# Part one of a fused attention and FFN kernel: one staggered sequence of steps over eight rows in place of two groups of four

## The chip, the cores and the metric

The kernel runs on one core of one Trainium2 chip. A core has five engines with queues of their own: TensorE (matmul, called PE in the profile), VectorE (DVE), ScalarE (ACT), GpSimd (POOL) and SyncE (SP), which here only issues DMAs. The metric is the device time of one execution in microseconds. The kernel before takes 1943.8 us, the median of 3 runs (1938.8 to 1947.53).

## What is computed

The input x has 8 batch rows of 2048 tokens with 256 features. A layer of Nystrom attention (16 heads of 16, 64 landmarks) is followed by a token-shift FFN, each on the layer-normed input and each layer-normed and added back.

```python
q_l = q.reshape(B, H, M, denom, HS).sum(axis=-2) / denom      # landmarks, M = 64
k_l = k.reshape(B, H, M, denom, HS).sum(axis=-2) / denom
s1 = softmax(einsum('bhld,bhmd->bhlm', q, k_l))
s2 = softmax(einsum('bhmd,bhnd->bhmn', q_l, k_l))
s3 = softmax(einsum('bhmd,bhld->bhml', q_l, k))
z = swapaxes(s2) / (max_row_sum * max_col_sum)                # pinv(s2), 6 iterations
for _ in range(6):
    xz = s2 @ z
    z = 0.25 * z @ (13 * I - xz @ (15 * I - xz @ (7 * I - xz)))
out = (s1 @ (z @ (s3 @ v))) @ Wo + bo
```

## The kernel before

The program has two parts. **Part one** makes, for each of the 8 batch rows, the statistics of the layer norm of x, the landmarks of q and k, and the pseudo-inverse of s2. The landmarks and the inverse go to DRAM (`landmarks`, `inverse`). **Part two** goes over the rows again, 4 chunks of 512 tokens each, and computes everything else; its order is written out in the lists `PRO`, `BODY` and `LAST` (line 353 on). The change leaves part two as it is, but for its first steps.

"Row" below means a batch row. Part one takes the rows in two groups of GR = 4 (0 to 3, then 4 to 7). Row n uses set n % 4 of all buffers, with two of the eight PSUM banks, `pb[s][0]` and `pb[s][1]`, and one of three x1in buffers of 2 MB (NX1 = 3), so that a load of x waits for the pooling of the row three before. Within a group every stage is done for all four rows before the next stage begins:

- statistics of x (`st`, 4 quarters of 4 bn_stats each, then `mv` with 16 bn_aggr) on VectorE, the root on ScalarE (`ln`, `rstd`), pooling weights `pw` on VectorE, pooling by 16 matmuls on TensorE;
- the front: norm of the landmarks (`stl`, `mvl`, `xl`), transposes (`lT`, `xlT`), projections (`qk`, `ql`, `kl`, `lm`, `lmlo`), the block-diagonal q (`qbd`, two VectorE multiplies by head_mask, line 939), logits, softmax (`max`, `shift`, `exp`, `sum`, `rcp`, `X`), its transpose (`XT`), row and column sums (`cs` and the reduce at line 961), their maxima over a head (`cm`, `cg`, `cr`, `gb`, `gcol`), and X and XT multiplied by the factor (lines 999 and 1000, `gX`, `gXT`);
- 6 iterations of four phases, S, T2, T3 and Z with ZT. Each product is done in fp16 with high and low parts. ScalarE takes the high part of a PSUM bank (`high`, line 697), VectorE the low part (`low`, line 966), and copies then build the block-diagonal left operand of the next product: `Sbd` and `T3bd` (line 975, two copies of 64 partitions each) on VectorE, `ZTbd` (line 711, two as well) on ScalarE. TensorE multiplies in `product` (line 1243): 24, 48, 32, 24 and 24 matmuls for S, T2, T3, Z and ZT of one row. The last iteration has no Z and no ZTbd.

The statistics of rows 4 to 6 are spread over the iterations of rows 0 to 3 (`AHEAD`). Every engine has a list of steps (`pe_steps`, `act_steps`, `dve_steps`), and each step counts one semaphore of its engine up by one; `of(...)` gives the place in a list, on which the others wait. An engine executes its list strictly in order.

The inverses are written to DRAM from ScalarE's queue at the end of each group (line 728). At the end of part one ScalarE, VectorE and GpSimd wait for all lists that matter to them and for all landmarks and inverses to land in DRAM; SyncE too. TensorE waits only for ScalarE's and VectorE's lists. Then SyncE loads the first x chunks of part two (`stage_X`, line 488), VectorE normalises them (`stage_XA`, line 1046), TensorE transposes (`stage_R`, line 1336), and GpSimd clears buffers and sets the ones row of k_stack in four memsets on one partition (line 616).

Of the kernel before, what the change touches and what calls it, by code (L numbers as in the profile page):

```python
# [6 lines left out]
F16 = mybir.dt.float16  # L7
# [8 lines left out]
def sandwich(nc, x, Wk, Wq, Wv, Wo, bo, W_r, W_k, W_v, mu_r, mu_k, out):  # L16
# [23 lines left out]
    with ctx:  # L40
# [3 lines left out]
        def sem(name):  # L44
# [19 lines left out]
        ident16 = sb("ident16", [P, P], F16)  # L64
        eye7 = sb("eye7", [P, M], F16)
# [74 lines left out]
        p_pooled = sem("p_pooled")  # L140
        p_zero = sem("p_zero")
        p_pe = sem("p_pe")
        p_act = sem("p_act")
        p_dve = sem("p_dve")
        lm_out = sem("lm_out")
        zt_out = sem("zt_out")


        pe_steps = ([(n, s) for n in ("lT", "qk", "logits", "XT", "sums", "g") for s in ROWS]
                    + [(n, i, s) for i in range(ITERS) for names in (["S"], ["T2"], ["T3"], ["Z", "ZT"])  # L150
                       for s in ROWS for n in names if not (n == "Z" and i == ITERS - 1)])
        act_steps = ([(n, s) for names in (["ln", "rstd"], ["xlT"], ["ql", "kl", "lm"], ["exp"], ["XT", "XThi"],
                                           ["Zhi", "ZThi"])
                      for s in ROWS for n in names]
                     + [(n, i, s) for i in range(ITERS) for names in (["S"], ["ZTbd"], ["T2"], ["T3"], ["Z", "ZT"])
                        for s in ROWS for n in names
                        if not (n in ("Z", "ZT", "ZTbd") and i == ITERS - 1)])

        STATS = ([("st", 0), ("st", 1)] + [k for s in range(2, GR) for k in (("pw", s - 2), ("st", s))]
                 + [("pw", GR - 2), ("pw", GR - 1)])  # L160
        FRONT = [(n, s) for names in (["stl", "mvl", "xl"], ["lmlo", "qbd"], ["max", "shift"], ["sum", "rcp", "X", "rs"],
                                      ["cs", "XTlo", "XTbd"], ["cm", "cg", "cr", "gb"], ["gcol", "gX", "gXT"],
                                      ["Zlo", "ZTlo"])
                 for s in ROWS for n in names]
        PHASES = (["Slo", "Sbd"], ["T2lo"], ["T3lo", "T3bd"], ["Zlo", "ZTlo"])


        def stat_steps(s):
            return [("st", s, q) for q in range(NQ)] + [("mv", s)]

# [1461 lines left out]
```

## Time and profile before

| | us |
|---|---|
| median of 3 runs | 1943.8 |
| the profiled execution | 1952.56 |
| its span | 1950.8 |
| last VectorE step of part one ends | about 479.7 |
| transposes of part two begin | 499.73 |
| VectorE busy, whole span | 1439.3 (74%) |
| TensorE busy, whole span | 1590.1 (82%) |
| ScalarE busy, whole span | 984.0 (50%) |
| GpSimd busy, whole span | 254.0 (13%) |

Busy times of TensorE are modelled from pipelined matmuls. In a timeline, a line "x2" stands for two instructions in a row, and its length goes from the start of the first to the end of the last; what stands in square brackets is the idle time before them and who ended it. A mean of 680 ns for one instruction is longer than the distance from one start to the next (600 ns) where instructions follow each other densely.

### The profile page before, as it was taken

What the parts mean: (1) busy time and instruction counts of PE and PEld (TensorE: products, weight loads), DVE (VectorE), ACT (ScalarE), POOL (GpSimd) and SP (SyncE); (2) the same over time, 40 slices, a digit from 0 to 9 for tenths busy, and PEclk for the clock granted to TensorE, in tenths of its full rate; (3) what the DMA queues carried; (4) which work ended last, traced back from release to release, by engine and by line L of the source; (5) the groups of instructions that cost most, each with busy time, mean ns of one, the idle gap of its engine ahead of it and who ended that gap; (6) DMA issues with size and microseconds to landing.
All of it is one profiled execution on the core that took longest, in us unless ns stands there. A gap on an engine that the chain in (4) does not pass through costs nothing. (4 is left out here: it accounts for less than half of the span.)

```text
span 1950.8 us, 50437 instructions
## 1 busy us (share of the span) xinstructions
PE 1590.1 (82%) x21132; PEld 1094.9 (56%) x21132; DVE 1439.3 (74%) x3164; ACT 984.0 (50%) x1599; POOL 254.0 (13%) x134
## 2 busy tenths in 40 slices
PE   2677865786568989989988998998899899888786
PEld 1567755776335557556555744655564465556454
DVE  6889859777763796688579668957966895795465
ACT  1277714774224646545554654456465445645542
POOL 4000000001200111112011101211110121120112
PEclk9789986989778999999999999999999999999888
DMA  6400020001221212112131212213121121311110
GB/s 213 141 3 3 3 74 4 3 3 46 56 58 30 66 51 70 51 50 77 32 87 52 70 50 51 75 33 87 51 69 50 51 77 33 87 41 46 34 33 33
DMA packets 125697, 104.60 MB, mean 54 GB/s; under 512 B 30368, under 2 KB 123424, under 8 KB 125472
## 3 DMA queue, kind: packets, MB, share of 16 engines
q1 hardware_dynamic: 124320, 99.29, 18.2%
q8 instruction: 168, 2.75, 0.6%
q10 hardware_dynamic: 1152, 2.10, 0.3%
q14 instruction: 57, 0.47, 0.1%
HBM read 56.23 MB, written 19.92 MB: 39 GB/s over the span
## 5 line engine op out<-in xcount | busy, mean ns | idle before, releaser
L797 ACT ACTIVATE p<-wide 128x1024 f32<-128x1024 f32 x128 | 124.0, 1021 | 123.5 <-PE wide L1517 122.8
L1094 DVE TENSOR_REDUCE m<-wide 128x16 f16<-128x1024 f32 x128 | 150.4, 1216 | 41.8 <-PE wide L1401 41.5
L1577 PE MATMUL bank<-wrT,xrT 128*128 128x256 f32 x512 | 142.5, 440 | 46.1 <-ACT vv L763 36.1
L774 ACT ACTIVATE e<-wide 128x1024 f32<-128x1024 f32 x128 | 124.4, 1021 | 81.7 <-PE wide L1434 70.4
L1577 PEld LDWEIGHTS bank<-wrT,xrT 128*128 128x128 f32 x512 | 111.6, 223 | 72.0 <-issue 40.0
L1086 DVE TENSOR_REDUCE m<-wide 128x2 f32<-128x1024 f32 x128 | 149.8, 1212 | 2.9 <-PE wide L1381 2.9
L641 POOL TENSOR_TENSOR ob<-ob,xm 128x1024 f32<-128x1024 f32 x32 | 77.0, 2405 | 475.1 <-DVE ob L299 475.1
L1557 PE MATMUL bank<-wo,oT 128*128 128x256 f32 x512 | 120.9, 390 | 6.2 <-DVE xT L1054 3.6
L1587 PE MATMUL acc<-xkT,wkT 128*128 128x512 f32 x256 | 120.1, 613 | 7.1 <-DVE xkT L1167 7.1
L1599 PE MATMUL bank<-wvT,ka 128*128 128x256 f32 x512 | 117.6, 383 | 1.3 <-ACT x2T L822 0.8
L625 POOL TENSOR_TENSOR xm<-yy,xres 128x1024 f32<-128x1024 f32 x32 | 76.1, 2378 | 326.1 <-issue 265.7
L635 POOL TENSOR_TENSOR xkT<-x2T 128x1024 f32<-128x1024 f32 x32 | 60.6, 1893 | 433.2 <-ACT x2T L822 433.2
L1557 PEld LDWEIGHTS bank<-wo,oT 128*128 128x128 f32 x512 | 96.4, 193 | 25.7 <-issue 8.2
L1599 PEld LDWEIGHTS bank<-wvT,ka 128*128 128x128 f32 x512 | 95.3, 190 | 16.2 <-issue 1.9
L1130 DVE TENSOR_TENSOR oT<-acc,oT 128x512 f32<-128x512 f32 x64 | 42.1, 681 | 78.9 <-ACT oT L808 78.9
L1453 PE MATMUL acc<-e,vv 128*17 128x64 f32 x4096 | 77.6, 224 | 25.0 <-ACT e L774 21.0
L1343 PE MATMUL bank<-xT,w 128*128 128x512 f16 x384 | 92.0, 391 | 3.8 <-ACT x2T L822 1.9
L1343 PE MATMUL acc<-xT,w 128*128 128x512 f16 x384 | 93.3, 395 | 1.5 <-DVE xT L1054 1.5
L830 ACT ACTIVATE sg<-bank 128x512 f32<-128x512 f32 x64 | 38.1, 597 | 108.9 <-PE bank L1577 89.4
L1365 PE MATMUL bank<-w,xT 128*128 128x256 f16 x768 | 89.2, 273 | 3.8 <-ACT x2T L822 2.8
L975 DVE COPY ST_bd<-ST_d 64x1024 f16<-64x1024 f16 x192 | 81.0, 422 | 11.5 <-DVE ST_d L966 0.5
L1453 PEld LDWEIGHTS acc<-e,vv 128*17 128x17 f32 x4096 | 62.0, 99 | 42.8 <-issue 28.6
(283 smaller groups left out, 3766.9 us busy)
## 6 DMA issues: line engine op xcount, KB each, us to landing
x1in<-in_L_attn_x SPq DMA_DIRECT2D x8, 2048.0 KB, 10.0
xin<-in_L_attn_x SPq DMA_DIRECT2D x32, 512.0 KB, 4.1
k_stack<-kh SPq DMA_DIRECT2D x256, 64.0 KB, 2.0
xres<-in_L_attn_x SPq DMA_DIRECT2D x32, 512.0 KB, 4.1
out<-ob SPq DMA_DIRECT2D x32, 512.0 KB, 5.3
k_stack<-kl SPq DMA_DIRECT2D x128, 64.0 KB, 2.0
q_stack<-landmarks SPq DMA_DIRECT2D x192, 4.0 KB, 1.6
inverse<-X ACTq DMA_DIRECT2D x8, 256.0 KB, 2.2
```

The source lines that it names most:

```text
L774: sc.activation(e3[w][:, :], wide[w][:, :], ACT.Exp).then_inc(wide_drained[w], 1)
L797: sc.activation(p1[:, 2 * j:2 * j + 2, :], wide[w][:, :].rearrange("p (a n) -> p a n", a=2), ACT.Exp).then_inc(wide_drained[w], 1)
L975: ins = v.tensor_copy(dst[r, :, :, j * M:(j + 1) * M], src[r, :, :, :])
L1086: v.tensor_reduce(m3[:, 2 * j:2 * j + 2, c], wide[j % 2][:, :].rearrange("p (a n) -> p a n", a=2), AX.X, ALU.max).then_inc(wide_drained[j ...
L1094: v.tensor_reduce(m1[:, tiles, 2 * w:2 * w + 2, :].rearrange("p t q x -> p q t x"), wide[w][:, :].rearrange("p (q t x m) -> p q t x m", q= ...
L1343: ins = mm(dst[o][:, :], w16[:, w, wt, k, o * P:(o + 1) * P], xT[:, xt, k, :], start=(i == 0), stop=(i == len(TERMS) - 1))
L1365: ins = mm(bank[j][:, t * A:(t + 1) * A], xT[:, xt, k, tok], w16[:, 2, wt, k, :], start=(i == 0), stop=(i == len(TERMS) - 1))
L1453: ins = mm(acc[k][32 * q:32 * q + HS + 1, j * M:(j + 1) * M], vv[:, 2 * i + w, h, :], e3[w][:, h * M:(h + 1) * M], start=(w == 0 and j == ...
L1557: ins = mm(dst, oT[:, k, tok], wo[:, k, :], start=(k == 0), stop=(k == KB - 1))
L1577: ins = mm(bank[j][:, t * A:(t + 1) * A], xrT[:, k, tok], wrT[:, k, :], start=(k == 0), stop=(k == KB - 1))
L1587: ins = mm(acc[o][:, :], wkT[:, k, o * P:(o + 1) * P], xkT[:, k, :], start=(k == 0), stop=(k == KB - 1))
L1599: ins = mm(bank[j][:, t * A:(t + 1) * A], ka[:, k, tok], wvT[:, k, :], start=(k == 0), stop=(k == KB - 1))
```

## The change

Part one becomes one sequence over all eight rows. The grouped loops are replaced by one list of steps for each engine, written out, in which the rows are staggered: row 0 first, then 2, 1 and 3; the fronts of rows 4, 6, 5 and 7 begin as soon as the buffer sets of rows 0, 2, 1 and 3 come free. SyncE has a list as well, for the loads of x, the landmarks and the inverses, which now go out on SyncE's queue, row by row. Row n still uses buffer set n % 4, and the three x buffers go by n % 3.

Some steps change engine: `qbd`, `gX` and `gXT` go from VectorE to GpSimd (a new list, `pool_steps`); `XTbd` goes from VectorE to ScalarE; of each `Sbd` the second half (`Sbd1`) goes to ScalarE, the first stays on VectorE. The row sums of X (a reduce over 512 elements) become rsum times rcp, 8 elements (`rs`).

At the seam, the x chunks 0 and 1 of part two are loaded during part one (`early.0`, `early.1`), after the last `pool` and `qk` steps; the two `stage_XA` of them follow VectorE's list directly, ahead of its waits for the others, and leave the head of `PRO`. The ones row of k_stack is written by one DMA from a constant `ones16`, on SyncE's queue, in place of the four memsets.

The lists are shown with their first lines only; a line of "..." marks what is left out.

```diff
-        dve_steps, act_order = [], []
-        for i in range(B // GR):
-            dve_steps += [(i, *k) for k in STATS[i] + FRONT]
-            for it in range(ITERS):
-                for ph, names in enumerate(PHASES):
-                    dve_steps += [(i, n, it, s) for s in ROWS for n in names if not (n == "Zlo" and it == ITERS - 1)]
-                    if i == 0:
-                        dve_steps += [(1, *k) for k in AHEAD[4 * it + ph]]
-        pe_steps = [(i, *k) for i in range(B // GR) for k in pe_steps]
-        roots = [("ln", GR - 1), ("rstd", GR - 1)]
-        for i in range(B // GR):
-            act_order += [(i, *k) for k in act_steps if len(k) == 2 and (k[0] not in ("ln", "rstd") or i == 0 or k in roots)]
-            for it in range(ITERS):
-                act_order += [(i, *k) for k in act_steps if len(k) == 3 and k[1] == it]
-                if i == 0 and 1 <= it < GR:
-                    act_order += [(1, "ln", it - 1), (1, "rstd", it - 1)]
-        act_steps = act_order
...
+        dve_steps = listed("""st0.0 st1.0 st3.0 st2.0 mv.0 st0.2 st1.2 pw.0 st3.2 st2.2 mv.2 st0.1 stl.0 pw.2 mvl.0 st1.1 xl.0
+            st3.1 stl.2 st2.1 mvl.2 mv.1 xl.2 lmlo.0 pw.1 st0.3 st1.3 stl.1 st3.3 max.0 mvl.1 shift.0 xl.1 st2.3
+            sum.0 mv.3 rcp.0 st0.5 max.2 X.0 shift.2 pw.3 rs.0 st0.4 sum.2 max.1 cs.0 XTlo.0 rcp.2 cm.0 X.2 cg.0
...
+            ZTlo.5.7""")
...
+        act_steps = listed("""ln.0 rstd.0 ln.2 rstd.2 xlT.0 ql.0 kl.0 lm.0 ln.1 rstd.1 xlT.2 ql.2 kl.2 lm.2 exp.0 xlT.1 ql.1 kl.1
+            lm.1 ln.3 rstd.3 exp.2 XT.0 XThi.0 XTbd.0 XT.2 XThi.2 xlT.3 exp.1 ZT0hi.0 XTbd.2 Z0hi.0 ql.3 kl.3
...
+        pe_steps = listed("""pool.0 pool.2 lT.0 qk.0 lT.2 pool.1 logits.0 qk.2 lT.1 qk.1 logits.2 logits.1 flip.0 pool.3 sums.0
+            flip.2 g.0 lT.3 sums.2 qk.3 g.2 flip.1 S.0.0 logits.3 sums.1 T2.0.0 S.0.2 g.1 T3.0.0 T2.0.2 Z.0.0
...
+        pool_steps = listed("""qbd.0 qbd.2 qbd.1 gX.0 gXT.0 qbd.3 gX.2 gXT.2 gX.1 gXT.1 gX.3 gXT.3 qbd.4 qbd.6 qbd.5 gX.4 gXT.4
+            gX.6 gXT.6 gX.5 gXT.5 qbd.7 gX.7 gXT.7""")
+        sp_steps = listed("""x.0 x.2 x.1 x.3 x.5 lmout.0 x.4 x.6 lmout.2 lmout.1 lmout.3 ztout.0 x.7 ztout.2 ztout.1 lmout.6
+            lmout.4 lmout.5 ztout.3 lmout.7 early.0 early.1 ztout.6 ztout.4 ztout.5 ztout.7""")
...
+            def step_early(c):
+
+                for n in range(B):
+                    sp.wait_ge(p_pe, max(of(pe_steps, "pool", n), of(pe_steps, "qk", n)))
+                sp.wait_ge(w16_lo, 3)
+                hold(sp)
+                load_x(0, c)
...
+            def step_ztout(n):
+                sp.wait_ge(p_dve, of(dve_steps, "ZTlo", ITERS - 1, n))
+                hold(sp)
+                sp.dma_start(zt_dram[bass.ds(n, 1)].rearrange("a p n -> p (a n)"),
+                             X[n % GR][:, :, :].rearrange("p a m -> p (a m)")).then_inc(zt_out[n % GR], 16)
...
+            sp.wait_ge(ones_made, 1)
+            sp.dma_start(k_stack[KS - 1:KS, :, :], ones16[:, :]).then_inc(ones_set, 16)
...
+            def step_qbd(n):
+                s = n % GR
+                pool.wait_ge(p_act, of(act_steps, "ql", n))
+                if n >= 2:
+                    pool.wait_ge(p_pe, of(pe_steps, "logits", n - 2))
+                for k in range(KB):
+                    ins = g.tensor_tensor(qbd[n % 2][:, k, :, :],
+                                          qlT[s][:, 0, k, :].unsqueeze(1).to_broadcast([P, HB, M]),
+                                          head_mask[:, :].unsqueeze(2).to_broadcast([P, HB, M]), ALU.mult)
+                ins.then_inc(p_pool, 1)
+
+            def by_sum(n, t):
+                pool.wait_ge(p_dve, of(dve_steps, "gcol", n))
+                g.tensor_tensor(t[:, :, :], t[:, :, :], gcol[n % GR][:, :].unsqueeze(2).to_broadcast([P, PAIRS, M]),
+                                ALU.mult).then_inc(p_pool, 1)
+
+            def step_gX(n):
+                pool.wait_ge(p_pe, of(pe_steps, "flip", n))
+                by_sum(n, X[n % GR])
+
+            def step_gXT(n):
+                pool.wait_ge(p_act, of(act_steps, "XThi", n))
+                pool.wait_ge(p_dve, of(dve_steps, "XTlo", n))
+                by_sum(n, XT[n % GR])
...
-            for c in range(NC):
-                if c:
-                    pool.wait_ge(ones_set, c)
-                g.memset(k_stack[KS - 1:KS, :, c * CH:(c + 1) * CH], 1.0).then_inc(ones_set, 1)
...
+            def blocks(dst, src, halves=range(2)):
+
+                act.wait_ge(p_zero, 3 * GR)
+                for j in halves:
+                    r = slice(j * HALF, (j + 1) * HALF)
+                    ins = sc.activation(dst[r, :, :, j * M:(j + 1) * M], src[r, :, :, :], ACT.Copy)
+                ins.then_inc(p_act, 1)
+
+            def step_XTbd(n):
+                act.wait_ge(p_dve, of(dve_steps, "XTlo", n))
+                blocks(XT_bd[n % GR], ST_d[n % GR])
...
+            def step_Sbd1(it, n):
+                act.wait_ge(p_dve, of(dve_steps, "Slo", it, n))
+                blocks(ST_bd[n % GR], ST_d[n % GR], [1])
+
+            def step_ZTbd(it, n):
+                act.wait_ge(p_dve, of(dve_steps, "ZTlo", it - 1, n) if it else of(dve_steps, "ZT0lo", n))
+                blocks(ZT_bd[n % GR], ZT_d[n % GR])
...
+            def step_rs(n):
+                s = n % GR
+                done("rcp", n)
+                v.tensor_tensor(rc1[s][:, 0, :], rsum1[s][:, :], rcp1[s][:, :], ALU.mult).then_inc(p_dve, 1)
...
+            def step_Sbd(it, n):
+                blocks(("Slo", it, n), ST_bd[n % GR], ST_d[n % GR], [0])
...
-        PRO = [("X", 0), ("XA", 0), ("X", 1), ("XA", 1), ("R", 0), ("X", 2), ("X", 3), ("Q", 0), ("AK", 0), ("XA", 2),
+        PRO = [("R", 0), ("X", 2), ("X", 3), ("Q", 0), ("AK", 0), ("XA", 2),
...
+            for c in range(2):
+                stage_XA(None, 0, c)
```

## Rows read from the trace of the kernel before

**Rows 1.** The head of the page, with busy time by engine.

```profile
span 1950.8 us, 50437 instructions
...
PE 1590.1 (82%) x21132; PEld 1094.9 (56%) x21132; DVE 1439.3 (74%) x3164; ACT 984.0 (50%) x1599; POOL 254.0 (13%) x134
```

**Rows 2.** Windows: stretch, length, busy us by engine (instructions), clock, DMA share, GB/s.

```profile
0.00:479.80 479.80, 324.85 (x7932) 294.28 (x7932) 381.27 (x899) 255.26 (x399) 23.65 (x28) 0.87 0.15 46
59.00:100.00 41.00, 22.09 (x235) 19.48 (x234) 36.61 (x79) 13.11 (x26) 0.00 (x0) 0.70 0.53 167
99.00:257.00 158.00, 123.07 (x3543) 116.14 (x3544) 137.77 (x317) 110.03 (x162) 0.00 (x0) 0.92 0.01 3
333.00:479.80 146.80, 117.44 (x3487) 112.08 (x3484) 114.84 (x212) 106.17 (x150) 0.00 (x0) 0.94 0.02 6
```

**Rows 3.** Waits up to 480 us: who for whom, total us, times, longest.

```profile
DVE ST_d L966 <- ACT ST_d L697: 37.6, 19, 4.9
```

**Rows 4.** Groups by form, VectorE, up to 480 us: total, mean ns, idle before.

```profile
L975 DVE COPY ST_bd<-ST_d 64x1024 f16<-64x1024 f16 x192 | 81.0, 422 | 11.5 <-DVE ST_d L966 0.5
...
L939 DVE TENSOR_TENSOR qbd<-qlT,head_mask 128x512 f32<-128x512 f32 x16 | 10.3, 686 | 4.8 <-PE bank L1276 4.4 <-PE wide L1276 0.3
...
L975 DVE COPY XT_bd<-ST_d 64x1024 f16<-64x1024 f16 x16 | 6.7, 421 | 0.9
L999 DVE TENSOR_TENSOR X<-X,gcol 128x512 f32<-128x512 f32 x8 | 5.5, 692 | 0.3
...
L961 DVE TENSOR_REDUCE rc<-X 128x8 f32<-128x512 f32 x8 | 5.5, 686 | 0.3
```

**Rows 5.** Timeline of ScalarE, iterations of rows 4 to 7: start, length.

```profile
360.86 8.56 ACT L711 ACTIVATE ZT_bd<-ZT_d 64x1024 f16<-64x1024 f16 x8
...
369.94 1.08 ACT L697 ACTIVATE ST_d<-wide 128x512 f16<-128x512 f32 x2
```

**Rows 6.** Timeline of VectorE in an iteration of rows 0 to 3.

```profile
116.64 1.28 DVE L966 SCALAR_TENSOR_TENSOR ST_d<-wide,ST_d 128x512 f16<-128x512 f32 x2
...
119.75 0.67 DVE L966 SCALAR_TENSOR_TENSOR ST_d<-bank,ST_d 128x512 f16<-128x512 f32 x1
120.52 0.86 DVE L975 COPY ST_bd<-ST_d 64x1024 f16<-64x1024 f16 x2
121.41 0.69 DVE L966 SCALAR_TENSOR_TENSOR ST_d<-wide,ST_d 128x512 f16<-128x512 f32 x1
```

**Rows 7.** Timeline of TensorE: one product of 24 matmuls, last iteration.

```profile
472.49 0.86 PE L1243 MATMUL bank<-ZT_d,ST_bd 128*128 128x64 f16 x24
```

**Rows 8.** Timelines at the start and at the seam, VectorE, GpSimd, TensorE, ScalarE.

```profile
9.32 5.33 DVE L899 BATCH_NORM_STATS2 st<-x1in 128x6 f32<-128x256 f32 x16 [2.10 <-DMA x1in<-in_L_attn_x]
...
21.24 5.33 DVE L899 BATCH_NORM_STATS2 st<-x1in 128x6 f32<-128x256 f32 x16 [5.28 <-DMA x1in<-in_L_attn_x]
...
479.04 0.68 DVE L1028 TENSOR_SCALAR X<-acc 128x512 f32<-128x512 f32 x1
482.37 0.06 DVE L1198 MEMSET x2T<- 128x2 f32 x1 [2.65 <-DMA inverse<-X]
486.17 14.60 DVE L1046 TENSOR_SCALAR xhat<-xin,mv,rstd 128x256 f32<-128x256 f32 x8 [3.74 <-DMA xin<-in_L_attn_x]
...
485.02 14.30 POOL L616 MEMSET k_stack<- 1x4096 f16 x4
...
499.73 1.94 PE L1336 MATMUL bank<-ident,xhat 128*128 128x128 f32 x8 [21.59 <-DVE xhat L1046]
...
500.94 0.60 ACT L742 ACTIVATE xT<-bank 128x512 f16<-128x512 f32 x1 [27.66 <-PE bank L1336]
```

**Rows 9.** Timeline of VectorE and GpSimd in part two, where both run.

```profile
710.44 3.42 DVE L299 TENSOR_SCALAR x2h<-xm,norm_m_mv,norm_m_rstd 128x256 f32<-128x256 f32 x4
...
748.78 1.37 DVE L299 TENSOR_SCALAR x2h<-xm,norm_m_mv,norm_m_rstd 128x256 f32<-128x256 f32 x4
...
710.61 2.45 POOL L641 TENSOR_TENSOR ob<-ob,xm 128x1024 f32<-128x1024 f32 x1 [12.13 <-DVE ob L299]
```

More of the change, by code:

```diff
@@ L143, in sandwich @@
         p_act = sem("p_act")
+        p_pool = sem("p_pool")
         p_dve = sem("p_dve")
[L145 to L165, printed above, removed]
@@ L195, in pm, with of @@
         def pm(t):
             return t.rearrange("p (a m) -> p a m", a=PAIRS)
[L198 to L200 removed]
+        def of(steps, *key):
+            return place[id(steps)][key]
         part2 = ctx.enter_context(ExitStack())
@@ new lines, in _ @@
+            step = {"ln": step_ln, "rstd": step_rstd, "xlT": step_xlT, "ql": step_ql, "kl": step_kl, "lm": step_lm,
+                    "exp": step_exp, "XT": step_XT, "XThi": step_XThi, "XTbd": step_XTbd, "Z0hi": step_Z0hi, "ZT0hi": step_ZT0hi,
+                    "Shi": step_Shi, "Sbd1": step_Sbd1, "ZTbd": step_ZTbd, "T2hi": step_T2hi, "T3hi": step_T3hi, "Zhi": step_Zhi,
+                    "ZThi": step_ZThi}
+            for key in act_steps:
+                step[key[0]](*key[1:])
+            act.wait_ge(p_pool, len(pool_steps))
@@ new lines, in _ @@
+            step = {"st0": quarter(0), "st1": quarter(1), "st2": quarter(2), "st3": quarter(3), "mv": step_mv,
+                    "pw": step_pw, "stl": step_stl, "mvl": step_mvl, "xl": step_xl, "lmlo": step_lmlo, "max": step_max,
+                    "shift": step_shift, "sum": step_sum, "rcp": step_rcp, "X": step_X, "rs": step_rs, "cs": step_cs,
+                    "XTlo": step_XTlo, "cm": step_cm, "cg": step_cg, "cr": step_cr, "gb": step_gb,
+                    "gcol": step_gcol, "Z0lo": step_Z0lo, "ZT0lo": step_ZT0lo, "Slo": step_Slo, "Sbd": step_Sbd,
+                    "T2lo": step_T2lo, "T3lo": step_T3lo, "T3bd": step_T3bd, "Zlo": step_Zlo, "ZTlo": step_ZTlo}
@@ L1038, in stage_XA @@
+            for key in dve_steps:
+                step[key[0]](*key[1:])
             def stage_XA(at, b, c):
@@ new lines, in step_Z, with step_ZT @@
+            def step_Z(it, n):
+                s = n % GR
+                pe.wait_ge(p_dve, of(dve_steps, "T3bd", it, n))
+                pe.wait_ge(p_act, of(act_steps, "ZTbd", it, n))
+                product(pb[s][1], ZT_bd[s], ST_d[s]).then_inc(p_pe, 1)
+            def step_ZT(it, n):
+                s = n % GR
+                pe.wait_ge(p_dve, of(dve_steps, "T3bd", it, n))
+                product(pb[s][0], ST_bd[s], ZT_d[s]).then_inc(p_pe, 1)
+            step = {"pool": step_pool, "lT": step_lT, "qk": step_qk, "logits": step_logits, "flip": step_flip,
+                    "sums": step_sums, "g": step_g, "S": step_S, "T2": step_T2, "T3": step_T3, "Z": step_Z, "ZT": step_ZT}
@@ L1320, in _ @@
+            for key in pe_steps:
+                step[key[0]](*key[1:])
+            pe.wait_ge(p_pool, len(pool_steps))
             pe.wait_ge(p_act, len(act_steps))
```

676 lines of the change are left out of this document (380 added, 296 removed).

## The prediction

> **What bounds the kernel now.** I first read the head of the page [rows 1]: VectorE is busy 74% and TensorE 82% of the whole span, which says nothing about part one. So I asked for busy times by stretch [rows 2]. Part one ends when VectorE ends, at 479.7 us [rows 8]. In it VectorE is busy 381.3 us (79%), ScalarE 255.3 (53%), TensorE 324.9 modelled (68%), GpSimd 23.7. The two stretches of iterations (99 to 257 and 333 to 479.8 us) have VectorE at 87% and 78%; the fronts between them leave TensorE and ScalarE nearly idle. VectorE is what is nearest to full, and the rest of the time is lost because four rows march in step: when all four stand at the same stage, every engine waits for the same thing. The waits say so [rows 3]: 37.6 us of VectorE idle are waits for ScalarE's high half. The collisions behind them are in the ScalarE timeline [rows 5]: eight ZT_bd copies in a row take 8.56 us, and the high halves of T2 stand behind them.
>
> **What the change removes from VectorE.** From the groups by form [rows 4]: half of the Sbd copies, 48 of the 192 in the ST_bd group; the 16 XT_bd copies; the 16 qbd multiplies; 16 multiplies by gcol (the group shown and its twin on XT); and 8 row sums of 512 elements, replaced by multiplies of 8 elements. A pair of copies takes 0.86 us, so one is 0.43, and two dense instructions of 0.68 take 1.28, so one is 0.60 from start to start [rows 6]. That gives 48 x 0.43 = 20.6, 16 x 0.43 = 6.9, 16 x 0.60 = 9.6, 16 x 0.60 = 9.6 and 8 x (0.60 - 0.15, an estimate for eight elements) = 3.6: together 50 us. VectorE's busy time in part one falls from 381 to 331; with the gaps of about 0.03 to 0.1 us that dependent instructions leave (0.77 us from a low half to its copy, 0.89 from the copy to the next low half [rows 6]) its list occupies it about 341 us.
>
> **What it puts on the others.** ScalarE needs 1.07 us for the copy of one half (8.56 / 8; ZTbd has two of them) and 0.50 per high half [rows 5]. A row-iteration is now 5 x 0.50 + 2 x 1.07 (ZTbd) + 1.07 (Sbd1) = 5.71 us on ScalarE, against 0.77 + 0.45 + 0.60 + 0.77 + 0.89 + 2 x 0.60 = 4.7 us on VectorE. So within the iterations ScalarE becomes the fuller engine, and in the fronts VectorE stays it. The iterations of all rows are 8 x (6 x 5.71 - 3.14) = 249 us of ScalarE (a last iteration has no Z and no ZTbd), plus about 51 for the fronts (XTbd alone 8 x 2.14): 300 us. TensorE: 24 products take 0.86 us including the last one's drain [rows 7], some 29 ns each; 888 a row make 26 us, with the front about 36 us a row, 285 us in all at a clock near full. GpSimd gets 32 instructions of 512 elements; one of 1024 takes 2.45 us [rows 9], so about 1.2 each, 38 us spread over part one. GpSimd has nothing else there. In the chain of one row the qbd step costs 2.4 instead of 1.3 us and the two gcol steps 2.4 instead of 1.2; other rows' steps cover that.
>
> **The new part one, from the lists.** (a) Up to the first Slo (row 0) VectorE has 77 steps: 20 quarters of statistics (5.33 us a row, 1.33 each [rows 8]), four aggregations of 1.1, four pw, four stl/mvl/xl of 1.2 together, and the softmax and sums steps of three rows: 53 us. The first x arrives at 9.3 us and the second at 21.2 as now [rows 8]; between them only 6.6 us of work is ready, so 9.3 + 5.3 = 14.6 us stand in front of that sum. I add 3 for row 0's own chain: first Slo at about 71 us, against some 99 now. (b) From there to row 4's first Slo the lists hold 260 VectorE steps, 24 row-iterations and most of the fronts of rows 3 to 6, with the statistics: 166 us on VectorE, 151 on ScalarE. VectorE decides. (c) From row 4's first Slo to the end: 24 row-iterations and the rest of rows 5 and 7: 121 us on VectorE, but 24 x 5.71 - 4 x 3.14 + 7 = 132 on ScalarE. ScalarE decides. Without any wait that is 71 + 166 + 132 = 369 us.
>
> Now the waits. The chain of one row through an iteration, product to product, is 0.9 + 0.6 + 0.7 + 1.1 + 1.6 + 0.6 + 0.7 + 1.1 + 0.6 + 0.7 + 0.9 + 1.6 + 0.6 + 0.7 = 12.4 us, with hops about 13.4. Four rows in flight need 4 x 5.71 = 22.8 us of ScalarE, so there is slack of some 9 us a round; three rows (part of (b)) need 17.1, and statistics and fronts fill VectorE. The lists show 18 to 23 us of VectorE work between successive Slo of row 0. So no single row's chain should end last. But all orders are fixed, three engines are 73 to 87% full, and each late step is waited for by all behind it in its queue. The groups now in lockstep reach 87% on VectorE at best [rows 2]; interleaved rows should do better. I take 5% of (b) and (c), 15 us.
>
> **GpSimd beside VectorE.** The trace has two places where they collide [rows 9]. Four tensor_scalars that take 1.37 us take 3.42 while a GpSimd add of 2.45 us runs: 2.05 us lost in one collision. And at the seam eight of them take 14.60 us beside the k_stack memsets. But most VectorE work of part one reads PSUM with at most one input in SBUF; the copies ST_bd and the few steps with two SBUF inputs are about one in three. Per GpSimd instruction the loss lies between 0 and its own 1.2 us, so 0 to 38 us; with a chance of about a half of meeting such a step, and half of the instruction left then, 0.3 x 32 = 9 us. I take 9, and keep both ends. The Trainium skill, "SBUF — State Buffer", section "Who interferes with whom", speaks against this part of the change: the port pair that the two engines share is an exclusive lock for the whole instruction, taken by copies and tensor_scalars in two-port modes and by instructions with two SBUF inputs against a GpSimd instruction that reads SBUF. The trace agrees in that the delayed group lost nearly the length of the GpSimd instruction. By that rule taken at its worst, all 32 held, part one would pay the 38 us; it is rival B.
>
> So part one ends at 369 + 15 + 9 = 393 us, against 479.7: 87 us less.
>
> **The seam.** Now [rows 8]: VectorE ends at 479.7, the inverses have landed at 482.4, x lands at 486.2, then xhat takes 14.6 us beside the k_stack memsets (14.3 us), the transposes begin at 499.73 and ScalarE drains them from 500.94. After: the early loads wait only for steps that lie some 80 us before the end, and the last steps of VectorE's list are followed by 8 tensor_scalars of about 0.34, 2.7 us in all, with no GpSimd beside them. TensorE may transpose 1.5 us after the last step; ScalarE's first drain waits for the last inverse, 2.7 us after it as now. So ScalarE starts about 3.0 us after VectorE's end instead of 21.2: 18 us less. What could be late next is the q_bd load on SyncE's queue: it needs some 8 us after the inverses, and its reader comes 10 us after the first drain; it just fits. The ones row by DMA has no reader for tens of us. TensorE no longer stands idle 21.6 us before its first projections, which may keep its clock up; I count 1 us for that and up to 3 as bound. Seam: 19 us.
>
> **The sum.** 87 + 19 = 106 us off the profiled 1952.6 (span 1950.8), 1846.6; off the median of 1943.8 it gives 1838. Part two keeps its work and its order, so nothing should be given back.
>
> **Rivals.** A, compact: no waits in (b) and (c) and no collisions. Part one ends at 369, seam 21: 1943.8 - 111 - 21 = 1812. For it: the slack above. Against: not even the dense stretches of now come near 100% [rows 2]. B, holes: the full 38 us of GpSimd and twice the waits (30), part one at 437, seam 18: 1943.8 - 43 - 18 = 1883; half of that, part one at 420, 1866. For it: [rows 9], and the 8.56 us of ZT_bd copies [rows 5] now come row by row with Sbd1 between them, each in the way of another row's high half. C, the seam doesn't shrink (the early loads or the landing of the inverses bind): part one as forecast, 4 instead of 19: 1853. D, slower: TensorE's clock. At the front of now, where TensorE has many gaps, the granted clock was 0.70 against 0.92 and 0.94 in the iterations [rows 2]. If the staggered order turned TensorE's work into short bursts with gaps all along, its 285 us of work at full clock would need, from about 28 us on, more than 470 us once the mean clock falls under 285 / 470 = 0.61; the part would then end behind 498 us, which is where the seam's gain is used up. At the lower level, 0.5 (1.2 of 2.4 GHz), it is 28 + 570 = 598 us, 100 slower. Against it: TensorE's share rises from 68% to over 75%, which should hold the clock up.
>
> **How the numbers follow.** Forecast 0.60 (1820 to 1856, time 1838); A 0.13; B 0.18; C 0.05; D 0.04. A measurement of this kernel can tell about 0.5% (10 us) from no change. The range reaches from A to the inner half of B: 1810 to 1876. Faster by over 0.5%: 0.95, the same 0.01, slower 0.04.
>
> **What would show it.** Right: VectorE busy about 331 and ScalarE about 305 us up to the end of part one; the last step with X of row 7 near 393; first Slo near 71; the transposes of part two within 2 us of that end, the first drain within 3 to 4; granted clock above 0.85. GpSimd's effect would show in ST_bd copies that take more than their 0.42 us. It would be wrong if VectorE's idle after 71 us is well above 60 us, if ScalarE waits on VectorE and VectorE on ScalarE in turns (a chain), or if the time after the seam grows.

## The result, and the profile after

The changed kernel takes 1851.4 us (median of 4 runs, 1846.5 to 1859.6), the kernel before on the same chip 1941.3 (4 runs, 1936.1 to 1947.5): a ratio of 0.9535 with a 95% interval of 0.9499 to 0.9571, or 90 us less. The forecast was 1838, with a range of 1810 to 1876. The profiled execution of the changed kernel took 1859.6 us, the longest of its four, that of before 1952.6, so 93 us went there. Every figure below that is not a ratio or a median is of profiled executions.

The head of the page of the changed kernel, which answers to [rows 1]:

```profile
span 1857.9 us, 50685 instructions
...
PE 1575.4 (85%) x21132; PEld 1087.1 (59%) x21132; DVE 1370.3 (74%) x3068; ACT 1041.2 (56%) x1663; POOL 278.4 (15%) x163
```

VectorE has lost 69 us of busy time, ScalarE has 57 more and GpSimd 24 more. The windows of part one in the order of the prediction's three steps, in the columns of [rows 2] (up to row 0's first Slo, from there to row 4's first Slo, from there to the end, and all of it):

```profile
0.00:79.00 79.00, 47.35 (x404) 36.45 (x404) 58.98 (x209) 23.65 (x50) 37.62 (x41) 0.89 0.67 217
79.00:266.00 187.00, 149.30 (x3906) 138.83 (x3910) 153.03 (x380) 154.02 (x225) 15.17 (x14) 0.91 0.07 22
266.00:415.00 149.00, 121.15 (x3630) 114.96 (x3622) 112.16 (x216) 134.44 (x189) 6.72 (x6) 0.97 0.05 15
0.00:415.00 415.00, 317.81 (x7932) 290.25 (x7932) 324.17 (x803) 312.11 (x463) 59.50 (x61) 0.93 0.18 57
```

The first Slo comes at 78.7 us (forecast 71), row 4's first Slo at 266.2 (237 by the lists, before waits), and part one ends at 415.3 (393). In the last stretch ScalarE, not VectorE, is the fullest engine: 134.4 of 149 us. The granted clock of part one rose from 0.87 to 0.93. Both figures are upper bounds: the profiles have no record of the clock before 38 us (before) and 46 us (changed), and the column counts that time as 1.00. From 46 us to the end of part one it was 0.86 before and 0.92 after.

The wait of [rows 3] has not become less in total (37.6 us before); it is now made of many short ones instead of a few long ones:

```profile
DVE ST_d L1115 <- ACT ST_d L838: 42.4, 52, 2.1
```

The seam, which answers to the second half of [rows 8] (timelines: start, length, what):

```profile
414.56 0.69 DVE L1187 TENSOR_SCALAR X<-acc 128x512 f32<-128x512 f32 x1 [0.25 <-PE acc L1414]
415.29 2.67 DVE L1207 TENSOR_SCALAR xhat<-xin,mv,rstd 128x256 f32<-128x256 f32 x8
...
416.92 1.06 PE L1536 MATMUL bank<-ident,xhat 128*128 128x128 f32 x8 [2.40 <-DVE xhat L1207]
417.67 1.09 ACT L883 ACTIVATE xT<-bank 128x512 f16<-128x512 f32 x2 [6.21 <-PE bank L1536]
```

The eight xhat instructions take 2.67 us instead of 14.60, right behind the last step; the transposes begin 1.7 us and the first drain 2.4 us after VectorE's end, instead of 20.0 and 21.2. So the 93 us are made of three pieces: part one 479.7 to 415.3, 64.4 us; the seam 21.2 to 2.4, 18.8 us; and what comes behind the first drain, 1449.9 to 1440.2, 9.7 us. The last piece has the same work in both. In the twelve kernels below it lay between 1433.9 and 1448.1 us: 1442 to 1448 in the three with the whole old seam, 1434 to 1447 in the nine with a new one in part or whole. Its spread is as large as the difference, so I put none of the 9.7 us down to the change, and can't exclude some.

### The profile page after: what moved, and what is told of

Same layout as the page of the kernel before. It is cut to its first block and busy times, and to the rows that moved or that the text cites. A ratio compares the mean times of both kernels' runs of the same rounds, so it can differ in the third digit from the quotient of the medians.

```text
span 1857.9 us, 50685 instructions
## 1 busy us (share of the span) xinstructions
PE 1575.4 (85%) x21132; PEld 1087.1 (59%) x21132; DVE 1370.3 (74%) x3068; ACT 1041.2 (56%) x1663; POOL 278.4 (15%) x163
## 5 line engine op out<-in xcount | busy, mean ns | idle before, releaser
L1265 DVE TENSOR_REDUCE m<-wide 128x16 f16<-128x1024 f32 x128 | 150.6, 1218 | 39.9 <-PE wide L1601 39.6
L1757 PEld LDWEIGHTS bank<-wo,oT 128*128 128x128 f32 x512 | 96.4, 193 | 25.7 <-issue 8.3
L1301 DVE TENSOR_TENSOR oT<-acc,oT 128x512 f32<-128x512 f32 x64 | 42.2, 682 | 81.3 <-ACT oT L949 81.1
L1565 PEld LDWEIGHTS bank<-w,xT 128*128 128x128 f16 x768 | 72.9, 98 | 21.0 <-issue 5.3
```

The source lines that it names most:

```text
L1265: v.tensor_reduce(m1[:, tiles, 2 * w:2 * w + 2, :].rearrange("p t q x -> p q t x"), wide[w][:, :].rearrange("p (q t x m) -> p q t x m", q= ...
L1565: ins = mm(bank[j][:, t * A:(t + 1) * A], xT[:, xt, k, tok], w16[:, 2, wt, k, :], start=(i == 0), stop=(i == len(TERMS) - 1))
L1757: ins = mm(dst, oT[:, k, tok], wo[:, k, :], start=(k == 0), stop=(k == KB - 1))
```

## The experiments

Each number "end of part one" below is the end of VectorE's last step in the profile, and each "drain" the time from there to ScalarE's first drain of xT. Every kernel does all the work of the reference; where one does added work it is said. The changed kernel and the first three kernels below have the same part one, and it ended at 415.3, 415.6, 412.2 and 417.5 us. So a difference of up to some 5 us between two ends of part one can be the spread of single profiles.

### The seam, undone, by halves and alone

In the changed kernel the seam is built as it was before: both x loads and the ones row by GpSimd.

```
-            lmout.4 lmout.5 ztout.3 lmout.7 early.0 early.1 ztout.6 ztout.4 ztout.5 ztout.7""")
+            lmout.4 lmout.5 ztout.3 lmout.7 ztout.6 ztout.4 ztout.5 ztout.7""")
...
-            sp.dma_start(k_stack[KS - 1:KS, :, :], ones16[:, :]).then_inc(ones_set, 16)
+            for c in range(NC):
...
+                g.memset(k_stack[KS - 1:KS, :, c * CH:(c + 1) * CH], 1.0).then_inc(ones_set, 1)
```

> The changed kernel with its whole seam undone: x chunks 0 and 1 loaded and normalised after part one, the ones row by four memsets. In the changed kernel ScalarE's first drain (L883) starts 2.4 us after VectorE's last step of part one, in the kernel before 21.2 us. Theory (the seam is worth that difference, whatever part one is): the drain starts about 21 us after the end again, and the time is 19 us above the changed kernel, ratio to before 0.963. Rival (most of the gain is part one, and part two swallows the seam's share later): the drain is 21 us late, but the time grows by under 8 us, ratio 0.954 to 0.957.

Measured: ratio 0.9657 (0.9605 to 0.971), part one ends at 415.6, the drain comes 20.9 us later. In the timelines of that kernel:

```profile
420.58 14.31 POOL L730 MEMSET k_stack<- 1x4096 f16 x4
421.98 14.34 DVE L1209 TENSOR_SCALAR xhat<-xin,mv,rstd 128x256 f32<-128x256 f32 x8 [4.00 <-DMA xin<-in_L_attn_x]
```

So the seam alone is worth 18.5 us (20.9 - 2.4). Next, only the first hunk (late loads, ones by DMA), then only the second (early loads, ones by memset).

> The changed kernel, only the early x loads undone; the ones row still by DMA, so no GpSimd memset stands beside the normalisation. Theory (most of the old seam is the collision of tensor_scalars with the k_stack memsets, 14.6 us for what takes 2.7): inverses land at 2.4 us, x 3.7 us later, four tensor_scalars 1.4 us, transposes and drain 1.2: drain at about 9 us after the end, 6.5 us above the changed kernel, ratio 0.957. Rival (the load is the larger part): drain at 15 us or more, ratio 0.961 or more.

Measured: 0.9592 (0.9554 to 0.9631); x landed 7.3 us after the end, xhat took 2.84 us, the drain came at 10.1 (about 9 expected). The load's latency is thus 7.7 us of the seam, and the collision the other 11.

> The changed kernel, only the ones row back on four GpSimd memsets of 3.5 us. Theory: the first two normalisations are over before the memsets begin, so the first drain stays at 2.4 us; the memsets run from about 5.5 to 20 us after the end, and the four tensor_scalars of chunk 2 (1.4 us now, at 11 us after the end) meet them and take about 7 us; the time grows by 0 to 6 us, ratio 0.9535 to 0.957. Rival (memset and tensor_scalar don't collide, the old 14.6 us had another cause, such as fresh x data): chunk 2 keeps its 1.4 us, no change.

Measured: 0.9588 (0.9562 to 0.9613), drain at 2.4 us. The collision moved to the next tensor_scalars that met the memsets:

```profile
428.49 9.02 DVE L1209 TENSOR_SCALAR xhat<-xin,mv,rstd 128x256 f32<-128x256 f32 x4
```

Four of them took 9.0 us instead of 1.4, and xT of chunk 1 was drained 24.4 us after the first drain instead of 14.0. I had expected about 7 us for the four and at most 6 us of added time; by the ratios it is 10 us, with intervals that just overlap. Early loads without the DMA for the ones row thus lose 10 us of their gain two steps later. The kernel before with the new seam alone:

> The kernel before with the seam alone: early loads of x chunks 0 and 1, their normalisation ahead of VectorE's waits, ones row by DMA; part one as before. Theory (seam and part one add up): first drain about 2.5 us after the end instead of 21.2, 19 us less, ratio 0.990. Rival (the seam's gain needs the new part one): ratio 0.995 or more.

Measured: 0.9888 (0.9849 to 0.9928), the end of part one at 478.7, drain at 2.6. The seam is worth the same, about 19 us, on either part one.

### Part one: the order and the moves apart

First the staggered lists with all the moved work back on VectorE, and the old seam. Its list is that of the changed kernel with qbd, gX, gXT, XTbd and the row sums put in behind the steps they wait for, and

```
-                blocks(("Slo", it, n), ST_bd[n % GR], ST_d[n % GR], [0])
+                blocks(("Slo", it, n), ST_bd[n % GR], ST_d[n % GR])
```

> The staggered lists with all moved work back on VectorE (qbd, gX, gXT, XTbd, both halves of Sbd, the full row sums) and with the seam of before. qbd stands eight steps behind xl in VectorE's list, gX and gXT behind gcol, XTbd behind XTlo. VectorE's list then needs about 391 us. Theory (stagger and shift of work each give a part; VectorE fills up): part one ends at 391 + 15 + 25 us of waits = 430 us, against 479.7 in lockstep and 415 in the changed kernel; with 21 us to the first drain the time is about 1946 - 50 = 1897, ratio 0.974. Rival (the stagger alone does it, the moves are worth nothing because ScalarE took over the load): part one ends at 415 to 420, ratio 0.967. Rival (the moves are the gain, 50 us of VectorE work): part one ends at 465 or more, ratio 0.992.

Measured: 0.9815 (0.9781 to 0.9849). Part one ends at 444.5 us, 14 later than expected and between the theory and its second rival; first Slo at 91.2, row 4's first Slo at 295.0. The order alone takes 35 us of the 64. ("Order" includes that the inverses are written from SyncE's queue, row by row, and no longer from ScalarE's at the end of a group.)

Then the moves alone, on the four rows in step of the kernel before:

```
-                     + [(n, i, s) for i in range(ITERS) for names in (["S"], ["ZTbd"], ["T2"], ["T3"], ["Z", "ZT"])
+                     + [(n, i, s) for i in range(ITERS) for names in (["S"], ["Sbd1"], ["ZTbd"], ["T2"], ["T3"], ["Z", "ZT"])
```

> The kernel before, in lockstep and with its seam, with only the moves of work: qbd, gX, gXT on GpSimd, XTbd and the second half of Sbd on ScalarE, row sums by the small multiply. Theory (in lockstep the moved half copies land in ScalarE's queue right where VectorE already waited for it: 4.3 us per iteration ahead of ZTbd and the T2 high halves): part one ends at 465 to 475 us, 5 to 15 less than 479.7, ratio 0.992 to 0.997. Rival (the moved 50 us come off whatever the order): part one ends at 430, ratio 0.974.

Measured: 1.0225 (1.0194 to 1.0256), slower; part one ends at about 516 us, 36 later. The sign was wrong. ScalarE and then VectorE in one iteration of that kernel:

```profile
167.06 4.42 ACT L738 ACTIVATE ST_bd<-ST_d 64x1024 f16<-64x1024 f16 x4 [0.37 <-DVE ST_d L994]
171.51 8.55 ACT L748 ACTIVATE ZT_bd<-ZT_d 64x1024 f16<-64x1024 f16 x8
180.09 0.60 ACT L730 ACTIVATE ST_d<-bank 128x512 f16<-128x512 f32 x1
...
170.84 1.39 DVE L936 BATCH_NORM_STATS2 st<-x1in 128x6 f32<-128x256 f32 x4
180.72 0.69 DVE L994 SCALAR_TENSOR_TENSOR ST_d<-bank,ST_d 128x512 f16<-128x512 f32 x1 [8.48 <-ACT ST_d L730]
```

and the wait of the same kernel that answers to [rows 3]:

```profile
DVE ST_d L994 <- ACT ST_d L730: 107.8, 24, 10.8
```

All four rows give ScalarE their Sbd1 at once, the eight ZT_bd copies stand behind those, and the four T2 high halves behind both: 13 us of ScalarE, for the last 8.5 of which VectorE has nothing left to do. VectorE's busy time fell from 381 to 336 us, and its waits for this one reason grew from 37.6 to 107.8. Work moved off the fullest engine made this kernel slower: in lockstep the two engines take turns. One place in ScalarE's list was tried, all four Sbd1 ahead of all ZT_bd. Whether another one (Sbd1 row by row, or the T2 high halves ahead of the ZT_bd copies) would keep the moves' gain in lockstep, or take part of the staggered order's, was not tried.

The last of this group is the changed kernel with GpSimd's steps back on VectorE (early seam kept), which separates GpSimd's moves from ScalarE's.

```
-            sum.0 mv.3 rcp.0 st0.5 max.2 X.0 shift.2 pw.3 rs.0 st0.4 sum.2 max.1 cs.0 XTlo.0 rcp.2 cm.0 X.2 cg.0
+            xl.1 st2.3 sum.0 mv.3 rcp.0 st0.5 max.2 X.0 qbd.1 shift.2 pw.3 rs.0 st0.4 sum.2 max.1 cs.0 XTlo.0
```

> The changed kernel, only GpSimd's steps (qbd, gX, gXT) back on VectorE; the rest as changed. VectorE gains 19 us of work and loses 7.6 us of stretched steps (lmlo 0.68 us instead of 0.42, Z0lo 0.88 instead of 0.68). Theory (VectorE decides in the fronts, collisions are the smaller evil): part one 6 to 12 us longer, ends at 421 to 427; the stretched steps are back at 0.42 and 0.68. Rival (collisions and GpSimd's slower steps cost as much as the move saves): part one ends within 3 us of 415.

Measured: 0.9678 (0.9651 to 0.9704), part one ends at 437.1, 10 us beyond the expected range. Against the changed kernel it is 21.9 us later, against the staggered lists alone 7.4 us earlier. GpSimd's 32 instructions are thus worth the 19 us of VectorE work that they carry, and perhaps a little more. ScalarE's copies and the shorter row sums, which this kernel keeps and which together carry 31 us, brought little: the 7.4 us are near the spread of 5. For 12.7 of the 21.9 us the place is ahead of the first Slo (91.4 against 78.7). The steps that came back ahead of it (qbd of four rows, gX and gXT of two) take about 7 us on VectorE, and its steps are 4.2 us less stretched there. The rest is waits, and those of this kernel up to 92 us name the largest new one, two waits of 7.9 us together:

```profile
DVE qbd L1057 <- ACT qlT L763: 7.9, 2, 4.1
```

qbd must wait for ScalarE's scaled queries. On VectorE everything queued behind it waits too; on GpSimd only GpSimd's own few steps do. How much of the wait a later place for qbd in VectorE's list would have saved was not tried. The price of GpSimd was small: of VectorE's steps beside its instructions only some of those with two inputs in SBUF, and three block copies, stretched. The groups of the changed kernel:

```profile
L1115 DVE SCALAR_TENSOR_TENSOR Z_d<-XT,Z_d 128x512 f16<-128x512 f32 x8 | 7.1, 884 | 1.2 <-ACT Z_d L817 1.1
...
L1078 DVE TENSOR_TENSOR lm<-qlT,lm 128x256 f16<-128x256 f32 x8 | 5.4, 681 | 3.8 <-ACT lm L801 3.8
```

against 682 and 418 ns without GpSimd. Added over all steps of part one the stretch is 7.6 us (9 forecast), while the ST_bd copies kept their 0.42 us but for three of 144. The timelines show which steps it was: those that began while a GpSimd instruction was running, such as Z0lo of row 0, which began at 72.79 us beside a qbd that ran to 73.76 and took 1.53 us. Where VectorE had begun first its step kept its length and GpSimd's took 1.2 to 1.6 us instead of 1.04.

### TensorE's clock in the front

Ahead of the first Slo TensorE works in short pieces with waits between them. In the changed kernel (the second to fourth column: length, engine, line):

```profile
24.38 3.64 PE L1424 MATMUL bank<-x1in,pw 128*32 128x256 f32 x32 [6.93 <-DVE pw L1050]
30.46 3.64 PE L1424 MATMUL wide<-x1in,pw 128*32 128x256 f32 x32 [2.44 <-DVE pw L1050]
...
52.76 7.04 PE L1452 MATMUL wide<-qlT,qbd 128*128 128x64 f32 x32
```

For the last of these the profile has the clock, in the columns of [rows 2]:

```profile
53.00:62.00 9.00, 9.00 (x68) 8.59 (x71) 5.46 (x14) 2.07 (x7) 2.04 (x2) 0.50 0.01 3
```

For the pooling at 24 and 30 us it has no record; that TensorE was at its lower level there (1.2 of 2.4 GHz) is read from the lengths alone, which are twice those of the same matmuls below.

To see what that costs, 39 matmuls with no reader are put ahead of its steps (added work):

```
+            def step_warm(count, _):
...
+                for _ in range(count):
+                    ins = mm(pb[3][1][:, :], ident16[:, :], w16[:, 0, 0, :, :].rearrange("p k n -> p (k n)"), start=True,
```

> The changed kernel with 39 extra fp16 matmuls of 512 columns on TensorE (extra work, written to a PSUM bank that row 3 uses later) ahead of pool.0, pool.2, lT.0, qk.0, pool.1, qk.1 and logits.2. In the changed kernel the pooling of rows 0, 2 and 1 takes 3.64 us each, qk.0 2 x 1.95 and the logits of rows 2 and 1 7.04 us, twice what the same work takes at the higher level. Theory (TensorE at its lower level holds up the first fronts): with the engine kept busy these take 1.9, 2 x 1.06 and 3.9 us, and the first Slo comes at 73 to 75 instead of 78.7; part one 3 to 6 us shorter. Rival (VectorE's list decides there anyway, or the level doesn't rise): first Slo within 1.5 us of 78.7 or later by the extra work.

Measured: first Slo at 73.9, as expected, where the seven kernels with the same front have it between 76.5 and 81.1; the pooling products took

```profile
24.81 1.93 PE L1424 MATMUL bank<-x1in,pw 128*32 128x256 f32 x32
```

1.93 us instead of 3.64, and part one ended at 407.8. Of these 7.5 us 4.8 lie ahead of the first Slo; the others can be spread. The whole kernel's ratio was 0.954 (0.9509 to 0.9571), no different from the changed kernel's: 7 us in one profile are below what the timing can tell.

### What decides the last stretch

From row 4's first Slo to the end I had 132 us of ScalarE's work. It took 149.0 in the changed kernel, but also 149.5 in the staggered lists alone, where ScalarE has 28 us less, and 150.6 with GpSimd's steps on VectorE. So perhaps ScalarE does not decide. I took Sbd1 off it for these rows, all four and two of them:

```
-                blocks(("Slo", it, n), ST_bd[n % GR], ST_d[n % GR], [0])
+                blocks(("Slo", it, n), ST_bd[n % GR], ST_d[n % GR], range(2) if n in (4, 5, 6, 7) else [0])
```

> The changed kernel with one edit: for rows 4 to 7 VectorE copies both halves of ST_bd again, so ScalarE has 24 copies of 1.07 us less (25.7 us) in the last stretch and VectorE 24 of 0.43 more (10.3). Stretch: from row 4's first Slo to the end of part one. In the changed kernel it took 149.0 us, with 11.7 us of idle on ScalarE and 36.8 on VectorE; forecast 132. Theory 'ScalarE's work decides': its busy time falls from 137 to 112, VectorE's rises from 112 to 122.5, so VectorE now decides and the stretch takes 122.5 plus 10 to 15 of waits, 133 to 138 us; part one ends 11 to 16 us earlier, ratio about 0.947. Rival 'the fixed order and the rows' chains decide': in the two staggered kernels run so far with less work on ScalarE or more on VectorE this stretch took 149.5 and 150.6 us; it stays at 147 to 151, ScalarE's idle rises from 12 to 37, and the ratio stays at 0.953 to 0.955.

Measured: 0.9521 (0.9496 to 0.9546); the stretch took 145.7 us, the end of part one 409.7.

> The changed kernel with both halves of ST_bd copied by VectorE for rows 4 and 5 alone: 12 copies of 1.07 us less on ScalarE (12.8), 12 of 0.43 more on VectorE (5.2). Theory 'ScalarE's work decides': 137 - 13 = 124.5 busy on ScalarE, 117 on VectorE, and the same idle of 12 on ScalarE: stretch 136 to 140 us, the best split of the two, ratio about 0.948. Rival 'order and chains decide': 147 to 151 us, ScalarE's idle about 24, ratio 0.953 to 0.955.

Measured: 0.9525 (0.9491 to 0.956); the stretch took 150.9 us, the end 413.2. In both, "ScalarE decides" as I had written it fell: 25.7 us less of its work brought 3.3. That is small, but more than spread, since the four kernels with the same part one have this stretch at 148.9 to 149.6. (The expectations put ScalarE's busy time there at 137 us; by the window it is 134.4.) Windows of the stretch in the kernel with all four rows changed:

```profile
264.00:410.00 146.00, 119.96 (x3626) 113.22 (x3618) 124.60 (x241) 110.72 (x164) 6.46 (x6) 0.98 0.05 16
```

VectorE now has 124.6 of 146 us, and ScalarE, now with 31 us of idle up to its last step, waits mostly for TensorE, which waits for VectorE's copies. But a limit reached from one side only is not yet one that doesn't exist: the mirror image was still to be tried, ScalarE doing each of these 24 copies twice (added work, into a tile without reader).

```
+                if n >= GR:
...
+                    copies.append(sc.activation(twice[HALF:, :, :, :], ST_d[n % GR][HALF:, :, :, :], ACT.Copy)
```

> The changed kernel with added work: for rows 4 to 7 ScalarE makes each Sbd1 copy twice, the first time into a tile that nobody reads, so it has 24 more copies of 1.07 us (25.7 us) in the last stretch; nothing else changes. It mirrors the run that took those 24 copies off ScalarE and shortened the stretch by only 3.3 us (149.0 to 145.7). Theory 'corner': in the changed kernel ScalarE decides this stretch (137 of its 149 us), and VectorE's and TensorE's queues stand right behind it, so taking work off gains a few us and adding it costs nearly all: stretch 170 to 176 us, part one longer by 21 to 27, ratio 0.965 to 0.969. Rival 'the chains and the fixed order decide, ScalarE doesn't': the 12 us of ScalarE idle absorb the first copies and the rest is shared: stretch 150 to 162, ratio 0.954 to 0.961.

Measured: 0.9691 (0.9653 to 0.9729); the stretch took 174.1 us, 25.1 more for 25.7 us of added work.

```profile
264.00:438.00 174.00, 129.10 (x3626) 122.33 (x3618) 111.61 (x216) 156.67 (x212) 6.57 (x6) 0.92 0.05 14
```

So the changed kernel stands at a corner: from there on each us of ScalarE costs a us, and with less of its work the stretch stays at 146 to 151. What holds it there is not shown. VectorE with TensorE's queue would fit the waits; so would the fixed order of the lists, which were not planned anew for the lighter ScalarE. Of the two stretches that had made me doubt, the one of 149.5 us had VectorE as its fuller engine (127.6 busy, ScalarE 106.0), and the one of 150.6 ScalarE, with 134.0 busy as in the changed kernel.

The last run puts the two edits that shortened part one together (the 39 added matmuls, and Sbd1 of rows 4 to 7 on VectorE):

> The changed kernel with two edits together: the 39 extra matmuls of the front (part one ended at 407.8 with them alone) and both halves of ST_bd on VectorE for rows 4 to 7 (409.7 with that alone). If the two gains add, 415.3 - 7.4 - 5.6 gives an end of part one at 402 to 404 us, a total of about 1842 and a ratio of 0.947 to 0.949. Rival: the differences of part one between runs of one code (412.2 to 417.5) explain them, and the ratio stays at 0.952 to 0.954 with part one at 407 to 410.

Measured: part one ends at 402.2 us, as expected if the gains add (13 less than the changed kernel, and 10 less than the earliest of the four with its part one), and the profiled span is 1839.7. The ratio is 0.9503 (0.9475 to 0.9531), between the two expectations, lower than the changed kernel's 0.9535 but not apart from it by their intervals. It is the fastest kernel here by its median, 1846.6 us, and not shown to be faster.

## Why the prediction was right, and where it wasn't

**The mechanism.** That part one lost time to the rows in lockstep, beside VectorE's work, held: the staggered order alone gave 35 of the 64 us with VectorE's work unchanged, and without that order the moves, in the one place tried, cost 36. The prediction listed order and moves in one sum and never asked what each would do alone; the answer is that here the second depended on the first. In the sum 50 us of removed VectorE work stood like a gain of its own. By the runs in the staggered order GpSimd's share (19 us of work) gave 22, the share of ScalarE's copies and the shorter row sums (31 us) 7.

**(a) First Slo, 71 forecast, 78.7 measured.** From the first x at 9.2 us VectorE's list took 55 us (53) and its idle 14.3, of which 5.4 for the second x. What failed is the 3 us for row 0's own chain: up to its first S it goes over TensorE seven times, at first at the lower level. The windows of before [rows 2] had shown a clock of 0.70 in the old front, and I used it for a rival only and not for a term. The run with the added matmuls gives 4.8 of the 7.7 us to it, with a spread of a few us between profiles; the rest is in size what GpSimd stretched ahead of the first Slo (lmlo, Z0lo, pw and rs, 4.2 us together, for which the forecast had its separate 9) and short waits.

**(b) 166 forecast, 187.5 measured.** "VectorE decides" did not hold: VectorE is busy 153 us and ScalarE 154. The term that was mis-sized is the waits, 5% by choice (8 us), 34 us measured on VectorE and 33 on ScalarE, 18%. The list itself had been put too long, 166 us against 153 busy, so the whole error of (b) is 13 us and not 26. The argument for 5% was that a row's chain of 13.4 us has slack against four rows' work. That compares one chain with one engine. With two queues each at 82% and in fixed order, an engine is idle whenever the other is late, and neither can take other work meanwhile. This is how I read the waits, and no run took them apart. Part of it is in one place, the fronts of rows 4 to 6 between 215 and 245 us: their pooling products and projections meet a TensorE at its lower level, with the iterations of row 3 queued behind them.

```profile
230.00:240.00 10.00, 9.68 (x86) 7.01 (x87) 6.00 (x27) 3.73 (x10) 2.22 (x2) 0.51 0.11 40
240.00:250.00 10.00, 10.00 (x199) 9.73 (x196) 8.41 (x20) 5.58 (x12) 2.24 (x2) 0.98 0.05 16
```

In these 20 us TensorE is full by the modelled busy time, VectorE busy 14.4 and ScalarE 9.3, and one T2 high half of row 3 waits 3.8 us for its product. What this place costs can be read from the other profiles, since nine kernels have the same lists in this stretch and differ in the clock that they were granted. With 0.91 over the stretch it took 187.5 to 187.7 us (the changed kernel and three others), with 0.92 or 0.93 184.4 to 185.0 (four), and with 0.94 183.5. The last is the kernel with Sbd1 of rows 4 and 5 on VectorE, whose clock stayed up here:

```profile
230.00:240.00 10.00, 8.93 (x161) 7.72 (x162) 9.28 (x35) 5.11 (x12) 2.22 (x2) 1.00 0.12 42
```

So by this comparison, which is not a controlled one, the lower level in this place makes at most about 4 of the 34 us; 30 remain without it.

**(c) 132 forecast, 149.0 measured.** ScalarE decides, as forecast, by the run that doubled its copies, and its sum was near: 134.4 us. The other 15 are 11.0 us of its idle where I had 6.6 for this stretch, and 3.8 us from ScalarE's end to VectorE's, since the last row's tail (low half, two block copies, one product, the last step) has nothing to overlap with; that tail was not in the sum. What the prediction didn't see is that the stretch is hardly worth relieving: it treated 132 against 121 as the margin, and with 25.7 us less of ScalarE's work the stretch was only 3 us shorter.

**Collisions with GpSimd, 9 forecast, 7.6 measured.** The guess of a third was right in size. The Trainium skill, "SBUF — State Buffer", section "Who interferes with whom", was weighed there for a loss of up to 38 us. Its finer rule, that a VectorE instruction with two SBUF inputs is held by a GpSimd instruction that reads SBUF and one with a single input outside the two-port modes is not, is what the groups show: lmlo and Z0lo stretched, the low halves that read PSUM did not. The worst case of rival B was not near: part one ended at 415.3 and not 437, though for another reason than collisions.

**The seam, 19 forecast, 18.8 measured**, with its two causes as given: 11 us of collision, 7.7 of load. The q_bd load, named as what could be late next, wasn't late: its reader starts 9.8 us after the first drain, at 427.5, and no engine waits for that load.

**The sum.** 87 + 19 was 106 off the profiled time; measured are 64.4 + 18.8, 83, and 9.7 more behind the seam that the spread of that stretch (14 us over all kernels) covers. By steps, part one ended 22 us later than forecast: 7.7 in (a), 13 in (b) with its waits, 10 in (c) with its waits, less the 9 us of collisions that were a term of their own and lie inside the three. That the total of 1851 came nearer to 1838 than part one did is then in part luck: the 9.7 us come from a stretch whose work is the same. By its part one the case is near the inner half of rival B, which had it end at 420; by its total it lies between the forecast and that. Rival A (no waits) is excluded by 71 us of VectorE's idle behind the first Slo, rival C (seam doesn't shrink) by the seam's runs, and rival D by the granted clock of 0.92 from 46 us on.

**The signs of being wrong.** Two of the three that the prediction named did show. VectorE's idle behind the first Slo is 71 us, where "well above 60" was to count against it. And the engines wait for each other in a chain, though over three engines: of the 66 us of waits that the profile lists for VectorE there, 56 are for ScalarE, and of ScalarE's 39 us 36 are for TensorE, which waits for the steps of both. The largest of ScalarE's:

```profile
ACT ST_d L838 <- PE wide L1414: 10.5, 14, 3.0
ACT ST_d L838 <- PE acc L1414: 8.9, 7, 3.8
ACT ST_d L838 <- PE bank L1414: 4.2, 6, 1.2
```

So the total was forecast well, and that 5% would do for the waits was not right. The third sign, a longer time behind the seam, did not show.

**What stays open.** In stretch (b) the copies on ScalarE and the shorter row sums took 18 us off VectorE (177.6 to 159.4 busy, staggered lists alone against the changed kernel with GpSimd's steps on VectorE) and 8.7 off the stretch; why only half came through was not tried. The waits of (b) were measured, not taken apart by a run, but for the 4 us of the clock.

## What to carry to other kernels

Before moving work to a second engine, look at what is queued there at that moment: with rows in lockstep all of them hand over at once, and the first engine waits for the last of it. Here the staggered order had to come first and the moves after it. A step that must wait for another engine is a good one to move to an idle engine, since that also frees the queue behind it: 19 us of such work gave 22 here, though each step took longer there. After the move, add up all the engines' sums for each stretch. In the two long stretches here, in fixed order, the fullest engine was idle for 18% and 10% of the time, and not 5, and in the second one relieving only that engine gave little.

## What was not expected of the hardware

- TensorE's two levels in short products: the same 32 matmuls of the pooling took 3.64 us at the lower level (by its length; the profile has no clock there) and 1.93 at the higher one, and a product of 16 small ones 3.5 (7.04 / 2, at a granted clock of 0.50) against 1.9. In a chain with little else to run, that was 4.8 us ahead of the first Slo; 39 more matmuls removed it.
- GpSimd memsets of 3.58 us each (14.31 / 4) on a single partition held VectorE's tensor_scalars of 0.34 us at 1.8 us each (14.34 / 8): two got through per memset. A region of one partition is enough to hold them; other sizes were not tried.
- Consecutive high halves on ScalarE (128 partitions) start 0.50 us apart though each is listed with 0.60; behind or ahead of a block copy on 64 partitions they hardly overlap. So ScalarE's busy share must be read from windows, not by adding up the means.
